# Attention heads of a low-rank path: the attend products in float32 over four column quadrants, and the softmax pipeline one head further ahead

## The reference, cut to what matters

```python
x = x + tanh(g_xattn) * experts(layernorm(x), ids, ctx)          # rows grouped by expert
h0 = layernorm(x)                                                # 4 batches of 512 tokens, width 512
attn = attention(rmsnorm(h0) * ln1_w, Wq, Wk, Wv, Wo)            # 16 heads of 32, causal, softmax
mod  = 0.1 * tanh(attn @ A)                                      # A: 512 x 16
h    = rmsnorm(h0) * ln2_w
gate = silu(h @ W_in.T + mod * (h @ A) @ B)
out  = x + tanh(g_ffn) * (h0 + (gate * (h @ W_up.T)) @ W_down.T) # inner width 2048
```

## Time and profile before

| | |
|---|---|
| time, median of 3 | 1033.87 us (1033.53 to 1034.25) |
| the profiled execution | 1034.01 us; its span, first to last instruction, 1032.3 us |
| busy, share of the span | PE 97%, PE weight loads 81%, DVE 68%, ACT 59%, POOL 27% |
| granted TensorE clock, mean | 0.998 of full |
| chain that ended last | PE 86%, POOL 6%, DVE 5% |

### The profile page before, as it was taken

One profiled execution on the slowest core, in us unless ns is written; L12 is line 12 of the kernel. 1 busy time (PEld: TensorE's weight loads), 2 busy tenths in 40 slices (PEclk: granted clock), 3 DMA queues, 4 the chain that ended last, 5 costly groups with the idle time before them and its releaser, 6 DMA issues.

```text
span 1032.3 us, 16767 instructions
## 1 busy us (share of the span) xinstructions
PE 1006.2 (97%) x5140; PEld 831.6 (81%) x5141; DVE 703.2 (68%) x1841; ACT 604.1 (59%) x1447; POOL 279.5 (27%) x276
## 2 busy tenths in 40 slices
PE   6999999999999999999999999999999999999998
PEld 6787888877888888778888888778888887888886
DVE  7766756996665559985664489966655599754443
ACT  4464456996434448985344379963444499843332
POOL 4537124861000117640000148600001187300000
PEclk9999999999999999999999999999999999999999
DMA  6545124344232426434232354343334254222321
GB/s 233 194 161 173 41 100 117 82 93 163 92 91 91 132 60 183 95 111 147 91 92 91 113 159 93 77 166 96 94 100 145 58 157 101 84 82 91 91 91 52
DMA packets 47073, 115.78 MB, mean 112 GB/s; under 512 B 6800, under 2 KB 6800, under 8 KB 46096
## 3 DMA queue, kind: packets, MB, share of 16 engines
q1 hardware_dynamic: 43968, 105.06, 34.0%
q0 software_dynamic: 3040, 9.96, 2.8%
HBM read 76.46 MB, written 13.37 MB: 87 GB/s over the span
## 4 chain that ended last, share of the span: by engine, by line
PE 86%; POOL 6%; DVE 5%; DMA 1%; issue 1%; ACT 1%; SPq 0%; DVEq 0%
PE bank L537 67%; PE bank L800 6%; PE bank L737 6%; POOL big L493 3%; PE bank L703 2%; PE bank L842 1%; DVE big L1409 1%; PE bank L854 1%; POOL wqs L432 1%; PE bank L593 1%; DMA big<-in_x,gidx 1%; PE bank L608 1%; PE bank L771 1%; PE bank L651 1%; DVE wr L1440 1%
## 5 line engine op out<-in xcount | busy, mean ns | idle before, releaser
L537 PE MATMUL bank<-hT,wr 128*128 128x512 f32 x1488 | 358.1, 390 | 0.0
L537 PEld LDWEIGHTS bank<-hT,wr 128*128 128x128 f32 x1488 | 279.2, 188 | 60.6 <-issue 1.4
L537 PE MATMUL bank<-wr,actr 128*128 128x512 f32 (+1 forms) x1224 | 303.4, 397 | 0.8 <-issue 0.4
L537 PEld LDWEIGHTS bank<-wr,actr 128*128 128x128 f32 x1224 | 229.1, 190 | 49.2 <-issue 1.3
L493 POOL TENSOR_SCALAR big<-big,rr 128x256 f32<-128x256 f32 (+1 forms) x124 | 149.5, 1214 | 75.6 <-DVE rr L1415 75.2
L432 POOL TENSOR_TENSOR wqs<-wstage,wqs 128x512 fp32r<-128x512 f32 x32 | 43.2, 1360 | 433.6 <-ACT wqs L957 432.3
L1440 DVE SCALAR_TENSOR_TENSOR wr<-stream,lns,wr 128x256 fp32r<-128x256 f32 x256 | 121.7, 537 | 52.2 <-ACT wr L1069 52.2
L1042 ACT ACTIVATE big<-big,nb 128x512 f32<-128x512 f32 (+3 forms) x256 | 140.6, 560 | 9.3 <-DVE nb L1409 9.3
L1395 DVE TENSOR_TENSOR wr<-bank,wr 128x512 fp32r<-128x512 f32 (+1 forms) x224 | 125.7, 607 | 15.7 <-ACT wr L957 15.0
L957 ACT ACTIVATE wr<-bank 128x512 fp32r<-128x512 f32 (+1 forms) x224 | 110.6, 530 | 30.1 <-PE bank L537 17.8
L957 ACT ACTIVATE actr<-act_sb 128x512 fp32r<-128x512 f32 x64 | 40.4, 632 | 146.0 <-DVE act_sb L1454 146.0
(11 more groups left out here) (174 smaller groups left out, 991.1 us busy)
## 6 DMA issues: line engine op xcount, KB each, us to landing
stream<-in_wmlp SPq DMA_DIRECT2D x64, 512.0 KB, 4.1
stack<-wr SPq DMA_DIRECT2D x192, 128.0 KB, 2.3
stream<-in_wmlp SPq DMA_DIRECT2D x64, 256.0 KB, 2.7
big<-in_x SPq DMA_DIRECT2D x4, 1024.0 KB, 7.8
big<-y_rows SPq DMA_DIRECT2D x4, 1024.0 KB, 5.6
residual<-big SPq DMA_DIRECT2D x4, 1024.0 KB, 5.1
big<-residual SPq DMA_DIRECT2D x4, 1024.0 KB, 6.5
out<-big SPq DMA_DIRECT2D x3, 1024.0 KB, 4.8
```

The source lines that it names most:

```text
L537: mm = pe.matmul(dst, lhs(pl, k), rhs(pr, k), start=start and i == 0, stop=stop and i == n - 1, skip_group_check=skip)
```

## The change

The attend products read the transposed probabilities and the values in plain float32 with no split. Each product goes to a quadrant of 32 columns of the array, that is to 32 rows of the output bank: 16 rows hold the head's result, and the four quadrants hold four partial sums. From head 4 on the 1280 columns of a head are cut into six pieces (`PIECES`: quadrant, first and last column, key block), 320 columns for each quadrant. At the end a matmul with `gather_rows` adds the quadrants.

ACT copies two banks, DVE one; the lows and `values_of` are gone. PE's step makes turn h+1, all scores of h+4, attend h, filling. DVE's step: maxima of h+3, normalise h+2, copy of bank 5 of h. ACT's: exponentials of h+2, copies of h, normalise h+2 in seven of the heads (POOL scales block 0 in the other nine). Projection halves 0 and 1 are made ahead of the heads, the others two steps ahead; 8 of the 12 matmuls of the first gate product move into head steps 13 and 14. `load_y` waits for attend of head 15 instead of the last transposes. One of the two copies to `zst` moves to POOL.

```diff
+ACT_HEADS = (0, 1, 2, 3, 4, 5, H - 1)
+def pool_tiles(head):
+    return (1,) if head == H - 1 else (1, 2) if head in ACT_HEADS else (1, 2, 0)
+PIECES = ((0, 320, 512, 1), (2, 256, 512, 3), (0, 0, 320, 0), (1, 128, 448, 2), (3, 384, 512, 1), (1, 448, 512, 3))
-COPY_AT = {(0, 2): (2, 0), (1, 0): (2, 1), (1, 2): (3, 0), (2, 0): (3, 1)}
+COPY_AT = {(0, 0): (2, 0), (0, 2): (2, 1), (1, 0): (3, 0), (1, 2): (3, 1)}
+AHEAD = 4
...
 # SP, load_y
-                sp.wait_ge(p_turned, b * (H * 3))
+                sp.wait_ge(pv_done, b * H)
...
 # PE, turn_tiles
-                if not first and kt != 3:
-                    pe.wait_ge(pt_lo, (n - 1) * 3 + PART_OF[kt])
+                if not first and kt == 1:
+                    pe.wait_ge(pt_dve, n)
+                elif not first and kt != 3:
+                    pe.wait_ge(pt_act, n * 2 - (kt == 2))
...
 # PE, filling
-                project_part(b, head + 1)
+                if head < QH * 2 - 2:
+                    project_part(b, head + 2)
...
 # PE, head_step
+                def attend(kt, begin, end, quadrant):
+                    bk, col, _ = TURNED[kt]
+                    wide = R * min(2, H - head)
+                    return pe.matmul(bank[ATT][32 * quadrant:32 * quadrant + wide, begin:end],
+                                     vp_rows[:, kt, R * head:R * head + wide],
+                                     turned[j % 2][bk][:, col + begin - kt * P:col + end - kt * P],
+                                     start=head == 0, stop=False, skip_group_check=True)
+                def attend_all():
...
+                    pe.wait_ge(pt_act, n * 2 + 2)
+                    pe.wait_ge(pt_dve, n + 1)
+                    if head < QUADRANTS:
+                        for kt in range(TT):
+                            mm = attend(kt, kt * P, S, (kt + head) % QUADRANTS)
+                    else:
+                        for piece in PIECES:
+                            mm = attend(*piece)
+                    mm.then_inc(pv_done, 1)
                 if head < H - 1:
                     wait_probs(n + 1)
                     for kt in TURN_ORDER:
                         turn_tiles(n + 1, other, kt)
...
+                if head < H - AHEAD:
+                    scores(n + AHEAD, j % 2, stack_loads(b, head + AHEAD))
+                attend_all()
+                filling(b, head)
...
 # PE, batch, ahead of the heads and behind them
+                project_part(b, 0)
...
-                project_part(b, 0)
-                scores_last(b * H + 3, 1, stack_loads(b, 3))
+                scores(b * H + 3, 1, stack_loads(b, 3))
+                project_part(b, 1)
...
-                gate_product(0)
+                pe.wait_ge(at_low, b + 1)
+                pe.wait_ge(rows_made, 1)
+                pe.matmul(bank[SUM][0:R, :], gather_rows[:, :], ysb[:, :], start=True, stop=True).then_inc(at_sum, 1)
+                gate_part(0, 8, DT * len(PARTS))
...
-                pe.wait_ge(at_sum, b + 1)
                 up_product(1)
                 pe.wait_ge(zs_ok, b + 1)
+                pe.wait_ge(zs_copy, b + 1)
...
 # ACT, head_step
-                if q < NQ - 1 or j < QH - 1:
-                    exponentials(n + 1, q * QH + j + 1)
+                if head < H - 2:
+                    exponentials(n + 2, head + 2)
                 if (q, j) in COPY_AT:
                     split_qk(b, *COPY_AT[q, j])
-                for i, (bk, w, at) in enumerate(TURNED_BANKS):
-                    act.wait_ge(p_turned, n * 3 + i + 1)
-                    copy(pts[:, j % 2, HI, at:at + w], bank[bk][:, 0:w]).then_inc(pt_hi, 1)
-                    if i == 0 and (q < NQ - 1 or j < QH - 1):
-                        normalise(n + 1, q * QH + j + 1)
+                act.wait_ge(p_turned, n * 3 + 1)
+                copy(turned[j % 2][6], bank[6][:, 0:256]).then_inc(pt_act, 1)
+                if head + 2 in ACT_HEADS:
+                    normalise(n + 2, head + 2)
+                act.wait_ge(p_turned, n * 3 + 3)
+                copy(turned[j % 2][4], bank[4][:, :]).then_inc(pt_act, 1)
...
 # DVE, head_step
-                if one_more:
-                    normalise(n + 1, (j + 1) % 2)
+                if head < H - 3:
+                    maxima(n + 3, (j + 1) % 2)
+                if head < H - 2:
+                    normalise(n + 2, j % 2)
+                if head == H - 1:
+                    dve.wait_ge(ha_low, b + 1)
+                    v.tensor_tensor(haT, bank[LOW_RANK][0:R, :], att_low, ALU.add).then_inc(ha_ok, 1)
                 if (q, j) in COPY_AT:
                     qk_low(b, *COPY_AT[q, j])
-                if two_more:
-                    maxima(n + 2, j % 2)
-                for i, (bk, w, at) in enumerate(TURNED_BANKS):
-                    dve.wait_ge(pt_hi, n * 3 + i + 1)
-                    low(pts[:, j % 2, LO, at:at + w], bank[bk][:, 0:w], pts[:, j % 2, HI, at:at + w], pt_lo)
+                dve.wait_ge(p_turned, n * 3 + 2)
+                v.tensor_copy(turned[j % 2][5], bank[5][:, :]).then_inc(pt_dve, 1)
```

More of the change, by code:

```diff
@@ L1 @@
+import itertools
 from contextlib import ExitStack
@@ L509, in _ @@
                     weights_low(b, 1, which)
-                normalise(b * H)
                 weights_high(b, 2, 0)
                 weights_low(b, 2, 0)
+                normalise(b * H)
+                weights_high(b, 2, 1)
+                weights_low(b, 2, 1)
                 for q in range(NQ):
@@ L516, in _ @@
                             normalise((b * NQ + q) * QH + j + 1)
-                        if q == 0 and j == 0:
-                            values_of(b, 0)
-                        elif j == 2 and q < NQ - 1:
-                            values_of(b, q + 1)
                         if (q, j) in WEIGHTS_AT:
@@ L795, in head_step @@
                 head, other = q * QH + j, (j + 1) % 2
-                def attend(kt, part):
-                    _, _, at = TURNED[kt]
-                    at_row = 64 * (j // 2) + R * (j % 2)
-                    return pe.matmul(bank[ATT][0:3 * R, kt * P:S], vst[:, q % 2, kt, at_row:at_row + 3 * R],
-                                     pts[:, j % 2, part, at:at + S - kt * P], start=head == 0 and kt == 0 and part == HI, stop=False,
-                                     skip_group_check=True)
+                def attend(kt, begin, end, quadrant):
[6 more added lines that the diff above has]
+                def attend_all():
+                    if head == 0:
+                        pe.wait_ge(vpa_ok, b + 1)
+                        pe.wait_ge(vpb_ok, b + 1)
+                    pe.wait_ge(pt_act, n * 2 + 2)
[7 more added lines that the diff above has]
+                    mm.then_inc(pv_done, 1)
                 if head < H - 1:
@@ L838, in gate_product, with gate_part @@
                               lambda p, k: hT[:, p, k, :], DT, stop=False)
+            def gate_part(par, begin, end):
+                for i in range(begin, end):
+                    k, (pl, pr) = i // len(PARTS), PARTS[i % len(PARTS)]
+                    pe.matmul(bank[GATE[par]][:, :], wch[:, par, pl, k * P:k * P + P], hT[:, pr, k, :],
+                              start=i == 0, stop=False)
             def modulate(par):
@@ L1115, in batch @@
                 split_qk(b, 1, 1, SECOND_K)
+                exponentials(b * H + 1, 1)
+                normalise(b * H + 1, 1)
                 for q in range(NQ):
                     for j in range(QH):
+                        if q == NQ - 1 and j == QH - 1:
+                            act.wait_ge(ha_done, b + 1)
+                            act.wait_ge(y_stored, 16 * ITEMS)
+                            copy(att_low, bank[LOW_RANK][32:32 + R, :]).then_inc(ha_low, 1)
                         head_step(b, q, j)
@@ L1538, in batch @@
                               bank[VALUES[1]][:, :]).then_inc(vpb_ok, 1)
+                maxima(b * H + 2, 0)
+                normalise(b * H + 1, 1)
                 for q in range(NQ):
@@ L1543, in batch @@
                     down_low(b, par, par)
-                dve.wait_ge(ha_low, b + 1)
-                v.tensor_tensor(haT, bank[LOW_RANK][0:R, :], att_low, ALU.add).then_inc(ha_ok, 1)
-                dve.wait_ge(at_low, b + 1)
-                v.tensor_tensor(att_sum, bank[ATT][0:R, :], att_low, ALU.add).then_inc(at_sum, 1)
                 dve.wait_ge(mod_ok, b + 1)
@@ L1645, in _ @@
                     values_low()
+                elif i == 5:
+                    v.tensor_reduce(gather_rows[:, :],
+                                    ident[:, :].rearrange("p (k r) -> p r k", k=QUADRANTS)[:, 0:R, :], AXX,
+                                    ALU.add).then_inc(rows_made, 1)
                 elif i in (6, 7):
```

108 lines of the change are left out of this document (37 added, 71 removed).

## The result

The changed kernel takes 1097.12 us (median of 4 runs, 1096.2 to 1098.53) against 1033.86 beside it (4 runs, 1033.53 to 1034.25): the ratio is 1.0613, with a 95% interval of 1.0595 to 1.0631. It is 63 us slower, where 50 were forecast.

A forecast was written before the change was run, and what follows sets the result against it. Before, PE then DVE and ACT bound the heads; after, a serial ring from copy to copy. 1034.0 + 46 (four batches of 11.5) + 6 for loads = 1086, said as 1084 us; range 1062 to 1108.

The forecast's parts named there:

- The sign: Whole kernel: the change makes it slower, 1084 us said against a median of 1033.87.
- the forecast's own case: Whole kernel: the summed terms hold, giving a time between 1075 and 1092 us, chance 0.55.
- The ring of 4.43: Steps 0 to 12: DVE's bank 5 copy, PE's turn, scores, maxima, normalise and next copy run in series, 4.43 us a step.
- The long steps: Three stretches between steps 1 and 6: ACT's copy of q or k delays the bank copy, 6.22, 6.22 and 5.90 us.
- Ahead of step 0: Before the head loop: bank 5 is turned at 184.8 against 181.55, +3.2 us a batch.
- Step 12 to the end of head 15: Last head steps: 11.1 us where it was 11.3, -0.2 a batch.
- Behind head 15: Bank copy, sum of quadrants and 16 filler matmuls after the last head: 5.67 us against 5.45, +0.2 a batch.
- The loads: Chunk 2's load, queued behind `load_y`, comes 2.1 us late in three batches: 6 us.
- Attend: Attend products of each head: quadrants run at once, 0.65 us a head, 0.97 in heads 0 to 3.
- The first rival: Attend: quadrants run one after another, 2.25 us a head, about +17 more a batch, 1154 us; chance 0.14.
- The rival of mode changes: Attend: time is lost at each change between whole array and quadrants, two a head, 1092 to 1103 us; chance 0.13.
- The faster rival: Head steps: the ring does not bind, about -5 us a batch, 1014 us; chance 0.08, 0.06 faster by over 0.2%.

The follow-up runs named there:

- Experiment 1: Changed kernel with DVE's copy of bank 5 moved to the front of its step: 1051.29 us, ratio 1.0165.
- Experiment 2: Changed kernel with ACT's copy of q or k and DVE's low of it moved behind the bank copies of their step: 1069.4 us, ratio 1.0347.
- Experiment 4: Changed kernel with the loads of MLP chunks 2 and 3 issued ahead of `load_y` and `load_x`: 1091.43 us, ratio 1.0548.
- experiment 6: Changed kernel with all attend products in quadrant 0, and the final sum reading that quadrant alone: 1154.15 us, ratio 1.1162.
- experiment 5: Changed kernel with key block 2's two transposes repeated, 8 extra in heads 8 and 9 and 4 in each from head 10: 1101.19 us, ratio 1.0652.
- Experiment 3: Changed kernel with bank copies first on DVE and ACT, the copies of q and k last, low-rank copies behind head 15's step: 1042.63 us, ratio 1.0104.
- experiments 8 and 9: Experiment 3 plus five zero-adding quadrant matmuls in heads 1 to 5: behind attend (8, 1061.37 us) or between the half projection's matmuls (9, 1097.97 us).
- the control: Experiment 3 with five zero-adding quadrant matmuls behind attend in each of heads 1 to 5: 1061.37 us, ratio 1.0247.

## Why the prediction was right, and what it missed

The sign, the mechanism and the range held. The time came out 13 above the forecast of 1084, and above the interval of 1075 to 1092 that the forecast's own case had; that it lies in the range is owed to the width given to the other cases. By its steps:

- **The ring of 4.43.** 4.47 in the five plain steps that the low clock left alone, with DVE's idle time of 1.53 where 1.5 was said. Experiment 1 takes the ring apart and gets 3.35.
- **The long steps.** Pairs of 10.78 and 10.93 for 10.65. Experiment 2 takes only this away: 28 less. The prediction had 5.1 a batch for it (2 x 1.79 and 1.47 above the ring), 20 in all. The rest was not taken apart; part of it may be the clock's, whose mean rose from 0.986 to 0.995 in the profiled executions (two low stretches in the batches for eight).
- **Ahead of step 0.** 184.66 for 184.8.
- **Step 12 to the end of head 15.** 11.8 for 11.1; the terms that the prediction lists here add up to 10.9, so its sum is 0.2 a batch above its own terms. The changes of mode lie here on the path: in these heads the transposes stand right before attend and ten of them take 1.19 (251.60 to 252.79) in place of 1.01, and each filling takes 0.12 more than its sum.
- **Behind head 15.** 5.55 for 5.67.
- **The loads.** 2.1 was said, PE waited 1.79, 1.53 and 1.88. Experiment 4 shows it, 5.7 for three batches.
- **Attend.** 0.65 was said, 0.68 measured, 0.98 for 0.97 in heads 0 to 3. The first rival, one after another, was put at 1154; experiment 6 measures 1154.15 for it. That the two agree so closely is luck, since 1154 was built on a sum that is 11 below the measured time; its attend of 2.25 is right all the same, with 2.28 measured.
- **The term that is missing** from the sum: every duration was taken at the full clock. The eight low stretches cost what the rows at both levels give: a ring step of 5.34 (226.88 to 232.22) for 4.47, a pair of 11.56 for 10.63 (10.93 less the 0.3 by which attend is shorter from head 4 on), the twelve matmuls behind the load 4.44 for 2.86 (experiment 4). That is 0.9 in the heads, where seven of the eight lie, and 1.6 behind the load: 8 in all. The changes of mode account for some 4 (0.7 a batch behind step 12, 0.3 to 0.5 within the long steps), and the load for -1. Together 11, of the 12.5 between 64.5 and the 52 of the sum. This division is worked out from rows and not shown by an experiment; no run took the low clock alone away, and the one that was to (experiment 5) did not. The executions of one kernel, which differ in their clock, give bounds: a stretch lowers the mean by 0.0016 (3.4 us at half the clock, of 1097). Over the 60 executions of the changed kernel and the experiments, compared within each kernel, one stretch goes with about 1.3 us, an estimate from their spans and mean clocks, so eight with 10; but the changed kernel's own four (1096.8 at 0.986, 1094.5 at 0.989, 1095.5 and 1095.2 at 0.991) give only some 0.4, so eight with 3. The clock's share is thus 3 to 10.
- **The rival of mode changes** is half right. The price exists and is 0.30 a head. That its time, 1092 to 1103, holds the result is chance: in the changed kernel the ring hides most of the price (64 heads at 0.30 would be 19, some 4 are paid), and by the rows above the larger part of the excess is the clock's.
- **The faster rival** (1014) supposed that once no ring bound them the steps would be held by PE (3.71) and ACT (3.3). Experiment 3 removes the ring, and PE sets its steps at 4.30 and 3.99, with 0.25 for mode changes; from step 6 on a step takes 3.75, by the second ring (experiment 3). In its batch 0 steps 0 to 12 are 2.2 shorter than before, the start and the part behind step 12 about 0.5 longer each, and the wait for the weights, 1.85, takes the remaining 1.1. The batches behind it add 2.3, 1.5 and 2.7 against before, of which that wait is 1.85, 1.62 and 1.57. What the change saves on DVE and ACT was never the limit in the steps with a projection.

## What to carry to other kernels

When work is moved one stage ahead, write down the ring it makes: from each buffer's release, through every instruction queued in front of the next release, on all engines. Here the busy shares of DVE and ACT fell and the kernel became 6% slower, and one copy moved to the front of its queue gave most of it back. Do it again for each repair: moving ACT's copies to the front as well took away the waits behind a projection and made a second ring through ACT and POOL. Then price what separates two kinds of matmul and what a new idle time does to the clock; both lie outside the durations of single instructions, and rows of a kernel that has neither cannot show them.

## What the runs showed of the hardware

- Four float32 matmuls in four column quadrants run side by side: starts 0.01 apart, 0.68 for 1280 columns that take 2.28 in one quadrant, 3.4 times. For heads 0 to 3, with unequal pieces, 0.98 against 2.27 (190.87 to 193.14), 2.3 times. The Trainium skill, "TensorE: Matmul & The Clock Gate", Part 3 (Packing small matmuls), gives 2.38 for three tiles of columns; four balanced ones do better here.
- Each float32 quadrant matmul appears as two instructions (12 for six pieces), while the float32 transposes on the whole array count one each.
- A change from whole-array float32r products of 512 columns to a float32 quadrant product and back costs 0.30, with the weight loads that are not hidden there (experiments 8 and 9).
- The low clock (0.50) comes in stretches of about 3.4 us. In the changed kernel all eight begin 0.2 to 1.2 behind a matmul that ends idle time of 1.7 to 1.8 in all, in the control's batch 0 behind 1.92, 2.03 and 2.82. Yet not every such idle time is followed by one: 1.70 ahead of 222.41 and 1.88 ahead of 740.64 are not. What decides between them stays open.
